# Cross-attention with a routed feed-forward on one core: q from x loaded turned, rows of rstd and choice transposed on chip

## The reference

```python
q = einsum('bsd,hdk->bhsk', layernorm(x), wq) + bq      # 16 heads of 8
k, v = the same of ctx with wk, wv
out = softmax(((q k^T) * 8**-0.5) v, axis=-1)           # softmax over the 8 features of a head
x1 = x + heads(out) @ wo.T + bo
t = rmsnorm(layernorm(x1)) * norm_w
weights = top 2 of softmax(t @ gate.T) over 8 experts, renormalised
h1 = t @ w1.T + 2 * (t a1_e) b1_e ;  h3 likewise        # low-rank part per expert e
out_e = (silu(h1) * h3) @ w2.T + 2 * ((silu(h1) * h3) a2_e) b2_e
x1 + sum_e weights_e * out_e
```

## Time and profile before

| | |
|---|---|
| runs | 298.67, 298.48, 297.51 us, median 298.48 |
| profiled execution | 297.54 us, its span 295.8 us |
| busy in the span | PE 285.6, DVE 224.1, ACT 187.6, POOL 180.8 us |
| granted clock of TensorE | 0.999 of full speed |
| DMA | 12.45 MB, mean 42 GB/s |

### The profile page before, as it was taken

The page is one execution under the profiler, slowest core; times in us unless marked ns, Lnnn a source line. Parts: engine busy times, 40 slices in busy tenths (PEclk is TensorE's granted clock), DMA queues, the critical chain, the costliest instruction groups (busy, mean ns, idle before and its releaser), DMA issues. The chain is left out here.

```text
span 295.8 us, 4543 instructions
## 1 busy us (share of the span) xinstructions
PE 285.6 (97%) x1499; PEld 238.0 (80%) x1499; DVE 224.1 (76%) x610; ACT 187.6 (63%) x310; POOL 180.8 (61%) x183
## 2 busy tenths in 40 slices
PE   8779999999999999999999999999999999999995
PEld 6547788878888888888888888888888887878884
DVE  3878996986689658894589765895579965795694
ACT  2478967674945966757855868459656658555542
POOL 3376599198970889429990589608982389518400
PEclk9999999999999999999999999999999999999999
DMA  5720020100210021200221011200012000100001
GB/s 155 281 72 3 0 73 1 72 3 25 81 71 2 0 72 38 71 1 2 71 71 39 0 53 55 71 0 2 1 37 73 0 0 35 75 1 0 35 2 35
DMA packets 7225, 12.45 MB, mean 42 GB/s; under 512 B 1825, under 2 KB 3234, under 8 KB 7202
## 3 DMA queue, kind: packets, MB, share of 16 engines
q1 hardware_dynamic: 6768, 11.77, 11.5%
q10 hardware_dynamic: 434, 0.39, 0.4%
HBM read 10.03 MB, written 2.13 MB: 41 GB/s over the span
## 5 line engine op out<-in xcount | busy, mean ns | idle before, releaser
L1010 ACT ACTIVATE silu<-h_ps 128x512 f32<-128x512 f32 x64 | 37.5, 597 | 33.2 <-PE h_ps L642 31.7
L1681 POOL TENSOR_TENSOR um_lo<-umf,um_hi 128x1024 fp32r<-128x1024 f32 x7 | 16.9, 2409 | 60.4 <-ACT um_hi L1002 60.4
L642 PE MATMUL h_ps<-um_hi,b_hi 128*128 128x512 f32 x128 | 51.4, 401 | 0.0
L642 PE MATMUL h_ps<-um_lo,b_hi 128*128 128x512 f32 x128 | 50.3, 393 | 0.6 <-DVE um_lo L1330 0.6
L642 PE MATMUL h_ps<-um_hi,b_lo 128*128 128x512 f32 x128 | 49.9, 390 | 0.0
L1343 DVE TENSOR_TENSOR act_second<-silu,h_ps 128x512 f32<-128x512 f32 x32 | 21.7, 680 | 17.2 <-PE h_ps L642 15.3
L1343 DVE TENSOR_TENSOR act_first<-silu,h_ps 128x512 f32<-128x512 f32 x32 | 21.4, 680 | 15.9 <-ACT silu L1010 12.7
L1703 POOL TENSOR_TENSOR scaled<-act_second,ratio 128x512 f32<-128x512 f32 x23 | 29.8, 1297 | 1.3 <-DVE act_second L1343 1.3
L642 PEld LDWEIGHTS h_ps<-um_lo,b_hi 128*128 128x128 f32 x128 | 24.0, 188 | 7.1 <-DVE um_lo L1330 1.4
L1002 ACT CAST um_hi<-umf 128x1024 fp32r<-128x1024 f32 x14 | 14.8, 1054 | 23.2 <-DVE umf L1324 22.2
L642 PEld LDWEIGHTS h_ps<-um_hi,b_lo 128*128 128x128 f32 x128 | 24.1, 188 | 4.5
(11 more groups left out here) (294 smaller groups left out, 793.0 us busy)
## 6 DMA issues: line engine op xcount, KB each, us to landing
chosen<-choice_dram SPq DMA_DIRECT2D x7, 512.0 KB, 3.5
x_in<-in_x_dram SPq DMA_DIRECT2D x7, 256.0 KB, 2.9
ctx_in<-in_ctx_t_dram SPq DMA_DIRECT2D x7, 256.0 KB, 3.2
out_dram<-y SPq DMA_DIRECT2D x7, 256.0 KB, 2.0
act_second<-in_hidden_w_dram SPq DMA_DIRECT2D x1, 512.0 KB, 4.3
act_second<-in_lora_w_dram SPq DMA_DIRECT2D x1, 512.0 KB, 5.4
v_parts<-in_down_w_dram SPq DMA_DIRECT2D x1, 512.0 KB, 4.8
ctx_in<-in_ctx_t_dram ACTq DMA_DIRECT2D x2, 128.0 KB, 3.2
```

The source lines that it names most:

```text
L642: mm = nc.tensor.matmul((h1_ps, h3_ps)[s][n % 2][:], b13[w][:, s, c * P:(c + 1) * P], um[k][m][:, s, :], start=False, stop=(i == 2), skip_ ...
L1010: nc.scalar.activation(silu[:, n % SILU_RING, :], h1_ps[n % 2][:], ACT.Silu).then_inc(silu_done.sem, 1)
L1681: nc.gpsimd.tensor_tensor(um[1][1][:], umf[1][:], as_f32(um[1][0][:]), ALU.subtract)\
```

## The change

For blocks 2 and later q no longer comes from normalised x. The host passes x also turned (`x_t`) and a centring matrix; the kernel multiplies the centring matrix by wq once (`center_queries`, `wqc_sb`), loads `x_t` per block by DMA into `xn_t`, and multiplies it directly (`turned_queries`, which replaces `turn_x`, `normal_x`, `x_turned` and `queries` there). The tokens' rstd is a row then: GpSimd computes it into a 128x32 pad (`turned_rstd`, two steps instead of four), VectorE transposes 32x32 squares of the pad (`turn_rstd`), SP writes it to DRAM in four DMAs and reads it back spread over the partitions (`spread_rstd`, `rstd_rows`), VectorE scales q by it (`scale_queries`), and ScalarE adds the bias in place (`bias_queries`). q's bank is `even_ps` instead of `odd_ps` from block 3 on, so `tail` waits for `q_scaled` and `turned_queries` for the residual `x1_done`.

`choice` is transposed in the same way (`turn_choice`), written in four DMAs instead of one, and returns in rows by word, so that gaps are read with unit stride and indices as every second bf16.

Cut to its core (declarations, semaphores, the host's two arrays and the moved calls that stand below are left out):

```diff
         gap = sb("gap", [P, TILES])
-        choice = sb("choice", [P, CHOICE])
-        chosen = sb("chosen", [P, P * CHOICE])
-
-        sb("spacer", [P, 8])
-        choice_index, choice_gap = choice[:, 0:INDICES // 2].bitcast(BF16), choice[:, INDICES // 2:]
+        choice = sb("choice", [P, SQUARE])
+        choice_t = sb("choice_t", [P, SQUARE])
+        chosen = sb("chosen", [P, CHOICE * P])
+        choice_index, choice_gap = choice[:, 0:INDICES // 2].bitcast(BF16), choice[:, INDICES // 2:CHOICE]
         row_expert_sb = sb("row_expert_sb", [P, 1])
...
         def q_bank(n, i):
-            return pair_a[i] if n == 0 else h1_ps[1] if n < AHEAD else odd_ps
+            return pair_a[i] if n == 0 else h1_ps[1] if n < AHEAD else odd_ps if n == AHEAD else even_ps
...
         def chosen_index(k):
-            words = chosen[:].bitcast(BF16).rearrange("q (p c) -> q c p", c=2 * CHOICE)
-            return words[:, k * TILES:(k + 1) * TILES, :]
+            words = chosen[:].bitcast(BF16).rearrange("q (c p k) -> q c p k", c=CHOICE, k=TOP)
+            return words[:, 0:TILES, :, k]
         def chosen_gap():
-            return chosen[:].rearrange("q (p c) -> q c p", c=CHOICE)[:, INDICES // 2:, :]
+            return chosen[:, INDICES // 2 * P:]
...
+            def load_xt(n):
+                sp.wait_ge(q_mm.sem, q_mm.of(n - 1))
+                sp.dma_start(xt_in, x_t[:, n * BLK:(n + 1) * BLK]).then_inc(xt_loaded, 16)
+
+            def spread_rstd(n):
+                sp.wait_ge(rstd_turned, turned(n))
+                rows_out = rstd_dram[n % 2].rearrange("(c a p) -> a c p", c=TILES, p=SQUARE)
+                for a in range(P // SQUARE):
+                    sp.dma_start(rows_out[a], rstd_t[a * SQUARE:a * SQUARE + TILES, :]).then_inc(rstd_out, 16)
+                sp.wait_ge(rstd_out, turned(n, 16 * (P // SQUARE)))
+                if n > AHEAD:
+                    sp.wait_ge(q_scaled, turned(n - 1))
+                sp.dma_start(rstd_rows[:], rstd_dram[n % 2].partition_broadcast(P)).then_inc(rstd_in, 16)
+
             def spread_choice(n):
-                sp.wait_ge(choice_done.sem, choice_done.of(n))
-                sp.dma_start(choice_dram[n % 2].rearrange("(p c) -> p c", c=CHOICE), choice[:])\
-                    .then_inc(choice_out.sem, 16)
+                sp.wait_ge(choice_turned.sem, choice_turned.of(n))
+                rows_out = choice_dram[n % 2].rearrange("(c a p) -> a c p", c=CHOICE, p=SQUARE)
+                for a in range(P // SQUARE):
+                    sp.dma_start(rows_out[a], choice_t[a * SQUARE:a * SQUARE + CHOICE, :]).then_inc(choice_out.sem, 16)
                 sp.wait_ge(choice_out.sem, choice_out.of(n))
...
                     pe.wait_ge(rows_ready, 1)
-                if n >= AHEAD + 1:
-                    pe.wait_ge(o_t_done.sem, o_t_done.of(n - 3))
-                elif n == AHEAD:
-                    pe.wait_ge(umf_done.sem, umf_done.of(0))
                 pe.wait_ge(xn_t_done.sem, xn_t_done.of(n, upto(i)))
                 nc.tensor.matmul(q_bank(n, i)[:, cols(i)], wq_sb, xn_t[:, cols(i)], start=True, stop=True)\
                     .then_inc(q_mm.sem, 1)
+
+            def center_queries():
+                pe.wait_ge(center_in, 16)
+                pe.wait_ge(kv_done.sem, kv_done.of(1, 1))
+                nc.tensor.matmul(h3_ps[0][:, 0:P], center_sb, wq_sb, start=True, stop=True).then_inc(wqc_mm, 1)
+
+            def turned_queries(n):
+                if n == AHEAD:
+                    pe.wait_ge(umf_done.sem, umf_done.of(0))
+                else:
+                    pe.wait_ge(x1_done.sem, x1_done.of(n - 1))
+                pe.wait_ge(xt_loaded, turned(n, 16))
+                nc.tensor.matmul(q_bank(n, WHOLE)[:], wqc_sb[:], xt_in, start=True, stop=True).then_inc(q_mm.sem, 1)
...
                     pe.wait_ge(heads_t_done.sem, heads_t_done.of(0, upto(i)))
-                elif n + 1 < BLOCKS:
-                    pe.wait_ge(q_t_done.sem, q_t_done.of(n + 1))
+                elif n == 1:
+                    pe.wait_ge(q_scaled, turned(n + 1))
                 else:
...
                     pe.wait_ge(y_done.sem, y_done.of(b - 1))
+                if b + 3 < BLOCKS:
+                    pe.wait_ge(q_scaled, turned(b + 3))
                 turn(y_bank, lambda t: o_t[:, t * P:(t + 1) * P]).then_inc(y_mm.sem, 1)
...
             gate(0, 1)
+            center_queries()
             first_base(1, 1)
...
                 if early:
-                    turn_x(b + 2)
                     keys_values(b + 2, 0)
                 hidden(b, 2)
                 project(b + 1)
                 hidden(b, 3)
                 b2_product(b - 1)
+                if early:
+                    turned_queries(b + 2)
                 hidden(b, 4)
-                if early:
-                    queries(b + 2)
                 tail(b - 1)
...
+            def centered_queries():
+                sc.wait_ge(wqc_mm, 1)
+                nc.scalar.copy(wqc_sb[:], h3_ps[0][:, 0:P]).then_inc(wqc_done, 1)
+
+            def bias_queries(n):
+                sc.wait_ge(q_scaled, turned(n))
+                nc.scalar.activation(q_t[:], q_t[:], ACT.Identity, bias=bq_sb[:, 0:1]).then_inc(q_t_done.sem, 1)
+
             def ctx_high(n):
...
                 sc.wait_ge(mask_scaled.sem, mask_scaled.of(n - 1))
-                nc.scalar.activation(tile4(ratio), chosen_gap(), ACT.Exp).then_inc(ratio_done.sem, 1)
+                nc.scalar.activation(ratio[:], chosen_gap(), ACT.Exp).then_inc(ratio_done.sem, 1)
...
                 early = b + 2 < BLOCKS
-                if early:
-                    normal_x(b + 2)
                 silu_step(b, 0)
                 silu_step(b, 1)
+                heads_turned(b + 1)
                 v_high(b - 1)
-                heads_turned(b + 1)
                 silu_step(b, 2)
                 silu_step(b, 3)
                 output_t(b - 1)
-                if early:
-                    x_turned(b + 2)
                 b_high(b, 0)
                 normal_tok(b + 1)
                 if early:
-                    queries(b + 2)
+                    bias_queries(b + 2)
                 silu_step(b, 4)
...
                     ve.wait_ge(var_done.sem, var_done.of(0))
-                elif n > 1:
+                elif n == AHEAD:
                     ve.wait_ge(shift_done.sem, shift_done.of(n - 1))
+                elif n > AHEAD:
+                    ve.wait_ge(var_done.sem, var_done.of(n - 1))
                 moments(x_in[n % 2], stats, mv, stats_done, mv_done, n, i)
+
+            def scale_queries(n):
+                ve.wait_ge(q_mm.sem, q_mm.of(n))
+                ve.wait_ge(rstd_in, turned(n, 16))
+                nc.vector.tensor_tensor(q_t[:], q_bank(n, WHOLE)[:], rstd_rows[:], ALU.mult).then_inc(q_scaled, 1)
+
+            def turn_rstd(n):
+                ve.wait_ge(rstd_done.sem, rstd_done.of(n))
+                if n > AHEAD:
+                    ve.wait_ge(rstd_out, turned(n - 1, 16 * (P // SQUARE)))
+                nc.vector.transpose(rstd_t[:], rstd_pad[:]).then_inc(rstd_turned, 1)
...
                 nc.vector.tensor_tensor(gap[:], top_l[:, :, 1], top_l[:, :, 0], ALU.subtract).then_inc(gap_done.sem, 1)
+
+            def turn_choice(n):
+                ve.wait_ge(choice_done.sem, choice_done.of(n))
+                if n > 1:
+                    ve.wait_ge(choice_out.sem, choice_out.of(n - 1))
+                nc.vector.transpose(choice_t[:], choice[:]).then_inc(choice_turned.sem, 1)
...
             act_step(0, 5)
+            turn_choice(1)
             first_weight(0)
             act_step(0, 6)
+            turn_rstd(3)
             mask_ktv(2)
...
                     keys_values(b + 2, 0)
+                    scale_queries(b + 2)
                 finish(b - 1)
...
                 act_step(b, 5)
+                turn_choice(b + 1)
+                if b + 3 < BLOCKS:
+                    turn_rstd(b + 3)
                 act_step(b, 6)
...
+            def turned_rstd(n):
+                pool.wait_ge(mv_done.sem, mv_done.of(n))
+                if n == AHEAD:
+                    pool.wait_ge(rstd_clear, 1)
+                else:
+                    pool.wait_ge(rstd_turned, turned(n - 1))
+                nc.gpsimd.tensor_tensor(var_eps[:], mv[:, :, 1], eps_ln[:], ALU.add).then_inc(var_done.sem, 1)
+                pool.wait_ge(var_done.sem, var_done.of(n))
+                nc.gpsimd.tensor_tensor(rstd_pad[:, 0:TILES], var_eps[:], minus_half[:], ALU.pow)\
+                    .then_inc(rstd_done.sem, 1)
+
             def rstd_x1(n):
...
                 pool.wait_ge(top_i_done.sem, top_i_done.of(n))
-                if n > 1:
-                    pool.wait_ge(choice_out.sem, choice_out.of(n - 1))
+                if n == 1:
+                    pool.wait_ge(choice_clear, 1)
+                else:
+                    pool.wait_ge(choice_turned.sem, choice_turned.of(n - 1))
```

(6 more changed lines are left out.)

56 lines of the change are left out of this document (42 added, 14 removed).

## The result

The changed kernel takes 300.99 us in the median of four runs (300.22 to 302.98), the kernel before 298.00 (298.48 in the three runs that the prediction had, and one more): a ratio of 1.0116, with a 95% interval of 1.0089 to 1.0144. It is slower by 1.2%; forecast were 296.3 us and a range of 294.8 to 298.1. The profiled execution took 300.71 us, with a span of 298.9.

The account below looks back on a forecast made before the run. The prediction took TensorE, busy in 97% of the span, to bound the kernel. Its terms -2.1, -0.4 and +0.6 sum to -1.9 us, giving a forecast median of 296.3 us, range 294.8 to 298.1.

Parts of the forecast that it names:

- Bound: Blocks 1 to 5: TensorE never waits, so work taken from its queue comes off the time one for one.
- Part 1: TensorE, blocks 1 to 5: four transposes a block go and the q product only moves; 0.42 us a block, 2.1 us saved.
- Part 2: New work on VectorE, ScalarE and GpSimd: scaling q (0.69 us) fits into an existing wait; nothing gained or lost.
- Part 3: Choice path: four writes, broadcast 0.6 us before the mask, second mask 0.5 us shorter; 0.4 us saved in the last block.
- both stalls: TensorE's waits at the first use of `um_lo`: 0.52 us in block 1, 0.39 in the last block; both forecast to go.
- Rival 1: Choice path: four writes run one after another, the mask waits 2.1 us, TensorE stalls at seven handovers; about 306 us, chance 0.10.
- Part 4: Opening, block 0: late rstd makes TensorE wait 1.3 us for `ktv`; less gains of 0.16 and 0.52, a loss of 0.6 us.
- The 0.16 us at the first `um_lo`: Block 0: TensorE comes 0.43 us earlier without its transposes, loses 0.27 waiting for the operand, and gains the rest.
- Sum: Whole kernel: -2.1 (blocks 1 to 5), -0.4 (last block), +0.6 (opening), together -1.9 us.

Follow-up runs that it names:

- e4_rstd_later: e1_old_places with VectorE's transpose of block 3's rstd moved, in pass 0, from in front of the masking of `ktv` to behind the shift of the scores: 297.62 us.
- h1_choice_later: e4_rstd_later plus ScalarE's old order, a VectorE wait before `um_lo`, new inputs declared last, and block 1's choice transpose moved behind the masking of `ktv`: 296.80 us.
- e1_old_places: The changed kernel with every tile that both kernels have put back at its SBUF address in the kernel before: 297.91 us, ratio 0.9997.
- e2_before_shifted: The kernel before with its spacer 192 bytes longer, so later tiles lie where the changed kernel has them; no instruction differs: 300.78 us, ratio 1.0108.

## Why the prediction was wrong

- **Bound.** Right that in a middle block TensorE is busy throughout, before and after. The step that failed is the one drawn from it: "work taken from its queue comes off the time one for one". It takes the pace of the work that is left as given. The transposes did come off, but the rest went from 0.227 to 0.233 us a product, and the middle block took 34.40 us, above the 34.2 that the prediction named as its own refutation. This is 3.5 us for the kernel at full clock (300.47 against 297.00 with the old places), and it decided the sign. The line that removes the spacer stood in the diff; neither a step nor a rival of the prediction mentions it.
- **Part 1.** Right: 0.45 us a block at equal places (forecast 0.42). The q product costs the same at both places.
- **Part 2.** Right in the middle blocks. A second step failed outside them: "ScalarE loses four normalisations [...] neither holds TensorE up", for which the sum has nothing. The lighter queue turned round who comes first in pass 0 (+0.59), and the new order of ScalarE's steps made `tok` late in block 6 (+0.52), where no early work covers it.
- **Part 3.** Right: writes 0.33 us apart (0.43 forecast), the broadcast issued 2.2 us behind the first of them (1.45 us behind the single write before) and landed 1.4 us ahead of the mask (0.6 forecast), second mask 0.75 us, both stalls gone. Rival 1 is refuted.
- **Part 4.** The stall before `ktv` was forecast at 1.3 and measured at 1.10 us, for a reason that was right in the smaller part: rstd's transpose makes 0.37 us (e4_rstd_later), the wait for the choice words 0.69 (h1_choice_later), on a GpSimd queue that binds next. The 0.16 us at the first `um_lo` were not to be seen.
- **Sum.** -1.9 forecast; at equal places -0.2 by the spans, and 0.0 at full clock (297.00 of e1_old_places against 296.98). The terms missed are the start (+0.5 against e2_before_shifted, +0.3 against the kernel before), `heads` (+0.6) and block 6 (+0.5). The last block gave 0.2 at the slower pace and 0.5 at the old places (forecast 0.4).
